# A GRU's input products: from seven products per four steps to 49 per eight

## The reference

```python
Xz, Xr, Xh = (x @ Wxg.T + bxg for g in "zrh")          # for all 512 steps
for t in range(512):
    Z = sigmoid(Xz[t] + H @ Whz.T + bhz)
    R = sigmoid(Xr[t] + H @ Whr.T + bhr)
    C = tanh(Xh[t] + (R * H) @ Whh.T + bhh)
    H = Z * H + (1 - Z) * C
    y[t] = H @ Whq.T + bhq
out = x + y
```

## Time and profile before

| | before |
|---|---|
| median of 3 runs, us | 2150.19 (2149.66 to 2152.09) |
| profiled execution: span, us | 2148.1 |
| PE busy | 2141.7 us, 100% |
| DVE busy | 1625.9 us, 76% |
| ACT busy | 914.6 us, 43% |
| POOL busy | 167.6 us, 8% |
| DMA | 62.20 MB, mean 29 GB/s |

### The profile page before, as it was taken

One profiled execution on the slowest core, in us unless ns is written; L12 is line 12 of the kernel. 1 busy time (PEld: TensorE's weight loads), 2 busy tenths in 40 slices (PEclk: granted clock), 3 DMA queues, 4 the chain that ended last, 5 costly groups with the idle time before them and its releaser, 6 DMA issues.

```text
span 2148.1 us, 179447 instructions
## 1 busy us (share of the span) xinstructions
PE 2141.7 (100%) x78028; PEld 2128.3 (99%) x78028; DVE 1625.9 (76%) x9472; ACT 914.6 (43%) x5118; POOL 167.6 (8%) x524
## 2 busy tenths in 40 slices
PE   9999999999999999999999999999999999999999
PEld 7999999999999999999999999999999999999998
DVE  5777777777777777777777777777777777777777
ACT  3444444444444444444444444444444444444443
POOL 1000000000000000000000000000000000000000
PEclk9999999999999999999999999999999999999999
DMA  4100010001000000000000100010001000010000
GB/s 155 29 24 24 26 29 24 24 24 31 24 24 24 29 26 24 24 26 29 24 24 26 29 24 24 25 30 24 24 24 30 25 24 24 26 29 24 24 26 27
DMA packets 111618, 62.20 MB, mean 29 GB/s; under 512 B 28786, under 2 KB 110834, under 8 KB 110834
## 3 DMA queue, kind: packets, MB, share of 16 engines
q1 hardware_dynamic: 111600, 61.98, 9.8%
q10 hardware_dynamic: 4, 0.02, 0.0%
HBM read 45.17 MB, written 16.78 MB: 29 GB/s over the span
## 4 chain that ended last, share of the span: by engine, by line
PE 99%; DMA 0%; DVE 0%; issue 0%; ACT 0%; POOL 0%; SPq 0%; DVEq 0%; POOLq 0%
PE gates L417 62%; PE p_bank L339 15%; PE gates L339 12%; PE y_bank L347 9%; PE p_bank L448 0%; PE gates L547 0%; DMA y_io<-in_x_res 0%; PE y_bank L540 0%; PE p_bank L540 0%; DMA out<-y_io 0%; DVE scanned L708 0%; DVE pre_t L644 0%; DVE wq_sums L698 0%; DVE y_io L648 0%; ACT scan_on L629 0%
## 5 line engine op out<-in xcount | busy, mean ns | idle before, releaser
L417 PE MATMUL gates<-wh,scanned 128*16 128x128 f32 x32768 | 1009.6, 273 | 1.5 <-DVE scanned L708 1.5
L417 PEld LDWEIGHTS gates<-wh,scanned 128*16 128x16 f32 x32768 | 933.4, 104 | 3.8 <-DVE scanned L708 1.3
L644 DVE STREAM_TRANSPOSE pre_t<-gates 128x32 f32<-128x32 f32 (+2 forms) x3584 | 617.1, 216 | 183.8 <-PE gates L417 139.3
L417 PE MATMUL gates<-wh,reset_state 128*16 128x128 f32 (+1 forms) x16384 | 562.0, 273 | 0.2 <-issue 0.2
L417 PEld LDWEIGHTS gates<-wh,reset_state 128*16 128x16 f32 (+1 forms) x16384 | 445.1, 103 | 0.5 <-issue 0.3
L614 ACT ACTIVATE r_gate<-pre_t 128x16 f32<-128x16 f32 (+1 forms) x1536 | 234.5, 215 | 408.4 <-DVE pre_t L644 408.4
L629 ACT ACTIVATE scan_on<-pre_t 128x16 f32<-128x16 f32 (+1 forms) x1536 | 236.4, 218 | 263.9 <-DVE pre_t L644 263.9
L339 PE MATMUL p_bank<-t,s 128*32 128x192 f32 x6096 | 333.9, 326 | 0.3 <-issue 0.3
L708 DVE TENSOR_TENSOR_SCAN scanned<-scan_by,scan_on 128x32 f32<-128x32 f32 x2048 | 299.3, 208 | 28.5
L617 ACT ACTIVATE scan_by<-pre_t 128x64 f32<-128x64 f32 x512 | 143.0, 279 | 263.9 <-DVE pre_t L644 263.9
L769 DVE TENSOR_TENSOR scan_on<-z_gate,scanned 128x64 f32<-128x64 f32 x512 | 120.8, 236 | 173.8 <-ACT z_gate L618 173.8
(11 more groups left out here) (77 smaller groups left out, 1538.5 us busy)
## 6 DMA issues: line engine op xcount, KB each, us to landing
y_io<-in_x_res SPq DMA_DIRECT2D x256, 64.0 KB, 1.9
out<-y_io SPq DMA_DIRECT2D x256, 64.0 KB, 1.6
xr<-in_x_t SPq DMA_DIRECT2D x127, 128.0 KB, 2.0
x_b<-in_x_t SPq DMA_DIRECT2D x127, 32.0 KB, 1.7
wx_v<-in_w_xv SPq DMA_DIRECT2D x1, 1536.0 KB, 6.5
wx_u<-in_w_xu SPq DMA_DIRECT2D x1, 1536.0 KB, 9.0
wh<-in_w_hr SPq DMA_DIRECT2D x1, 1024.0 KB, 10.7
wh<-in_w_hz SPq DMA_DIRECT2D x1, 1024.0 KB, 13.8
```

The costliest lines, as they stand in the source:

```text
L417: mm = nc.tensor.matmul(gate_rows(g, par, slice(Q * j, Q * j + rows)), of, w, start=False, stop=(m == G - 1), skip_group_check=True)
L644: nc.vector.transpose(flat(pre_t[g][:, a:b]), gate_part(g, par, a, b)).then_inc(done, 1)
```

## The change

A turn becomes eight steps (four pairs); 64 turns, of which two at the start and two at the end are unrolled on every engine, TensorE too, and 60 run in the loop. The x parts of a turn come from two levels of the scheme: seven products of blocks at the outer level, each again seven (49 block products, `x_products`), each over one m of 128 and 96 columns, four matmuls. The blocks 1, 2, 4 (`FIRST`) of the outer products are made in steps 4 to 7 of a turn, the others (`SECOND`) in steps 7 to 4 of the next; the results are used a turn later. The partial sums of the outer level pass through four banks by ACT copies (`start_a`, `a_to_b`, `d_to_b`, `d_to_c`, `z11_first` and so on; 14 per turn), DVE adds four (`z22_first`, `z12_first`, `z22_second`, `z12_second`, 288 or 384 columns). The inner level is put together on GpSimd from SBUF: 21 additions per turn (`combine_11`, `combine_21` of 96 elements, `combine_x2` of 192), next to four sums of x of 128 elements (`x_sum`) and four of 224 (`x_sub_sum`). ACT then copies the four pairs' parts to the gate banks (`put_u`, 256 columns, `put_v`, 128). Every GpSimd sum is issued behind a wait for a DVE event: the scans of a step (`after_state`), the state sums (`after_sums`), the third reset product (`after_reset`) or the kept product (`after_kept`). Gates lie in two banks for R and H (`u_bank`) and one for Z of both pairs (`v_bank`). The first eight pairs (16 steps) have plain products (`plain`), two gaps per pair. The 21 summed weight blocks of DVE (`sub_sum`) and 7 of GpSimd (`w_sub3`) are made during turns 0 and 1. The ten `keep_busy` matmuls between the first products are gone. SP loads 256 KB of x per turn of eight steps in one transfer.

```diff
-    W = P + P // 2
-    CW = G * W
...
+BLOCK = 96
+HALF = 2 * BLOCK
+COLS = 2 * HALF
...
-            turn(0, first=True, last=False)
-            with eng.Fori(1, turns - 1) as i:
-                turn(i, first=False, last=False)
-            turn(turns - 1, first=False, last=True)
+            turn(0)
+            turn(1)
+            with eng.Fori(2, turns - 2) as n:
+                turn(n)
+            turn(turns - 2, begins=False)
+            turn(turns - 1, ends=False, begins=False)
...
+            def x_sub_sum(n, k):
+                x = x_all[:, 0:7].rearrange("p s (i j q) -> p s i j q", i=2, j=2)
+                a0, a1, b0, b1 = (x[:, :, i, j, :] for i in range(2) for j in range(2))
+                s = {m: x_sub[:, m - 1] for m in range(1, 5)}
+                if n == 1:
+                    pool.wait_ge(s_ready[3], k + 1)
+                    pool.wait_ge(s_ready[4], k + 1)
+                    if not isinstance(k, int) or k > 0:
+                        pool.wait_ge(p4d_done, k)
+                    nc.gpsimd.tensor_tensor(s[1], b0, b1, ALU.add).then_inc(x_sub_made, 1)
...
+            def combine(op, made, z, x, k):
+                pool.wait_ge(made, 7 * k + op - 1) if op > 1 or not isinstance(k, int) or k > 0 else None
+                of = {1: (x(0, 0), z(1), z(2)), 2: (z(6), z(1), z(6)), 3: (z(3), z(5), z(3)),
+                      4: (x(0, 1), z(6), z(3)), 5: (z(7), z(6), z(7)), 6: (x(1, 0), z(7), z(4)),
+                      7: (x(1, 1), z(7), z(5))}[op]
+                nc.gpsimd.tensor_tensor(*of, ALU.add).then_inc(made, 1)
...
+                elif before:
+                    after_sums(2 * n)
+                    combine_x2(6, n - 2)
+                    combine_x2(7, n - 2)
+                    after_reset(t)
+                    combine_21(3, n - 2)
+                    after_kept(t)
+                    combine_21(4, n - 2)
+                    after_state(t + 1)
+                    combine_21(5, n - 2)
+                    combine_21(6, n - 2)
+                    after_reset(t + 1)
+                    combine_21(7, n - 2)
...
+                if begins:
+                    after_state(t + 5)
+                    x_sub_sum(1, n)
+                if ends:
+                    after_state(t + 5)
+                    combine_x2(1, n - 1)
+                    after_reset(t + 5)
+                    combine_x2(2, n - 1)
...
+            def x_products(to, a, blocks, only=None):
+                x, w = X_OF[a], W_OF[a]
+                x_raw = x_all[:, x].rearrange("p (i j q) -> p i j q", i=2, j=2)
+                for at, b in enumerate(blocks):
+                    if only is not None and at not in only:
+                        continue
+                    of = {1: x_raw[:, 0, 0], 2: x_raw[:, 0, 1], 4: x_raw[:, 1, 1], 3: x_sub[:, 3, x],
+                          5: x_sub[:, 0, x], 6: x_sub[:, 1, x], 7: x_sub[:, 2, x]}[b]
+                    by = {1: lambda: w_block(w, 0, 0), 2: lambda: w_block(w, 1, 0), 3: lambda: w_block(w, 1, 1),
+                          4: lambda: w_summed(4, w), 5: lambda: w_summed(1, w), 6: lambda: w_summed(2, w),
+                          7: lambda: w_summed(3, w)}[b]()
+                    for j in range(G):
+                        mm = nc.tensor.matmul(to[Q * j:Q * (j + 1), BLOCK * at:BLOCK * (at + 1)], of, by[:, j, :],
+                                              start=False, stop=True, skip_group_check=True)
...
+                    if s8 == 0 and ends:
+                        pe.wait_ge(z22a_out, n)
+                        x_products(a_bank, 4, FIRST).then_inc(p4a_done, 1)
+                        pe.wait_ge(b_put_d, n)
+                        if second:
+                            pe.wait_ge(w_sub3_made, 5)
+                        x_products(d_bank, 6, SECOND).then_inc(p6d_done, 1)
+                    elif s8 == 1 and ends:
+                        x_products(b_bank, 2, SECOND).then_inc(p2d_done, 1)
+                        pe.wait_ge(c_put_d, n)
+                        x_products(d_bank, 7, SECOND, (0,))
...
+                    elif s8 == 7 and begins:
+                        x_products(c_bank, 3, FIRST, (2,)).then_inc(p3a_done, 1)
+                        pe.wait_ge(b_started_a, n + 1)
+                        if first:
+                            pe.wait_ge(w_sub_made, 18)
+                        x_products(b_bank, 5, FIRST).then_inc(p5a_done, 1)
+                        pe.wait_ge(d_started, n + 1)
+                        pe.wait_ge(x_sub_made, 4 * n + 4)
+                        if first:
+                            pe.wait_ge(w_sub3_made, 1)
+                        x_products(d_bank, 1, SECOND).then_inc(p1d_done, 1)
...
+                    if s == 0 and (not static or n >= 2):
+                        put_v(par, x_part(p, n))
+                    if s == 0 and static and 1 <= 4 * n + p < 7:
+                        if 4 * n + p > 0:
+                            act.wait_ge(plain_done, 4 * n + p)
+                        put_u(1 - par, bias_rows)
+                        put_v(1 - par, bias_rows)
+                    if s8 == 0 and ends:
+                        p5_out_first(n - 1)
+                        d_to_b(n - 1)
+                    elif s8 == 1 and ends:
+                        d_to_c(n - 1)
...
+            def z22_first(k):
+                dve.wait_ge(p7a_done, k + 1)
+                dve.wait_ge(p5a_out, k + 1)
+                read_x2(k)
+                nc.vector.tensor_tensor(z_place(3, 0, 3), a_bank[:, 0:n_first], p5_first[:], ALU.add
+                                        ).then_inc(z22a_out, 1)
...
```

More of the change, by code:

```diff
@@ new lines, in keep_busy, with plain_in_gap @@
+                    nc.tensor.matmul(a_bank[Q * j:Q * (j + 1), :], zeros[:, 0:Q], zeros[:], start=True, stop=True)
+            def plain_in_gap(s8, t):
+                q = t // 2 + 1
+                if q >= 8:
+                    return
+                pe.wait_ge(z_turned, t + 1)
+                if q == 1 and t == 0:
+                    plain(1, 1, (0, 1))
+                    return
+                if q == 1:
+                    plain(1, 1, (2, 3)).then_inc(plain_done, 1)
+                    return
+                pe.wait_ge(u_put[q % 2], q // 2)
+                pe.wait_ge(v_put[q % 2], q // 2)
+                pe.wait_ge(x_rest_loaded, 16 if q < 4 else 32)
+                mm = plain(q, s8 % 2, range(G))
+                if s8 % 2 == 1:
+                    mm.then_inc(plain_done, 1)
@@ L537, in _ @@
             pe.wait_ge(zeros_ready, 1)
[L538 removed]
+            for to in (y_bank, c_bank, d_bank):
                 for j in range(G):
@@ L622, in turn @@
                         nc.scalar.copy(q16[:], y_bank[:, Q16_AT:Q16_AT + YW]).then_inc(q16_copied, 1)
-                    elif c == 1 and not last:
-                        if not first:
-                            act.wait_ge(ub_put, i)
-                        fill_p5()
                     for h, (a, b) in enumerate(PARTS):
@@ L712, in renew, with turn @@
                 mm.then_inc(state_ready[h], 1)
-            def turn(i, first, last):
-                for c in range(4):
-                    t = 4 * i + c
+            def turn(n, ends=True, begins=True):
+                static = isinstance(n, int)
+                first, second = static and n == 0, static and n == 1
+                last = not ends
+                ends = ends and not first
+                for s8 in range(8):
+                    odd, c = divmod(s8, 4)
+                    i, t = 2 * n + odd, 8 * n + s8
                     par, s = divmod(c, 2)
+                    end = last and odd == 1
+                    begin = first and odd == 0
                     old = state_before(c)
-                    if c == 0 and not first:
+                    if c == 0 and not begin:
                         state_sums(i)
-                    elif c == 1 and not first:
-                        put_ub(i)
-                    elif c == 2 and first:
+                    elif c == 2 and begin:
                         dve.wait_ge(q6_done, 1)
```

894 lines of the change are left out of this document (583 added, 311 removed).

## The result

The changed kernel takes **3002.73 us** (median, 3000.73 to 3004.05) against 2150.9 of the kernel before beside it: ratio **1.396 [1.394, 1.398]**, 852 us slower, where 405 slower was forecast. The profiled execution has a span of 2998.8 us at a mean granted clock of 0.932, where before had 1.00.

The account below looks back on a forecast made before the run. TensorE's records times columns bound the kernel, then its code loads. Span 2148.1 - 59 + 1 + 7 + 4 = 2101 with kept code, + 444 + 8 = 2553 with loads, plus 2.1 to the median: 2555 us, range 2102 to 2740.

Parts of the forecast that it names:

- The code: TensorE's loop body of 11 packets is loaded anew each pass: 7.4 us per body, +444 us over 60 bodies.
- Eleven need 36.3 us: TensorE's loop body: eleven code packets at 3.3 us each, where the body's work needs 32.2 us.
- another 3.3: TensorE's branch back aims at replaced code with nothing asked for ahead: one more load of 3.3 us per pass.
- Unrolled turns, +8: The four unrolled turns on TensorE load 42 packets of code: +8 us.
- +4: First sixteen steps: DVE's weight sums between its transposes delay H's transposes and others, +4 us (1 to 10).
- +7: Last eleven steps lose their products but must keep 1.05 us per gap: shortfalls sum to +7 us.
- Products, -59: TensorE's x products: 392 records of 96 columns replace 224 of 192 per eight steps, 583 to 524 us, -59.
- ScalarE hidden, transfers hidden: ScalarE's 22 copies per eight steps and SP's 256 KB x loads per body hide behind other work, costing nothing.
- GpSimd: Sums after the state sums (steps 0 and 4) delay DVE's reset products: 0.5 us per body, uncounted under code loads.
- A (2103): Whole kernel: code is kept and GpSimd's sums hold no one, 2103 us; chance 0.16.
- B (2134): Steps 0 and 4: code is kept, GpSimd's sums hold DVE's reset products, 31 us, giving 2134 us; chance 0.22.
- C (2277 to 2301): TensorE's loop: loads are just in time and only the branch back costs, 2277 to 2301 us; chance 0.12.

Follow-up runs that it names:

- loop of narrow records: No GRU computed: TensorE alone runs 16 passes of ten packets of 64-column matmuls on zeros; 175 packets in 619.3 us.
- loops of zeros: No GRU computed: TensorE alone runs loops of 16 passes of matmuls on zeros, varied in code size and columns; 3.54 us per packet with 64 columns.
- fitted half turn: Changed kernel, TensorE looping over four steps, branches picking x products, head at packet start, two y products left out: 2189.89 us, ratio 1.019.
- doubled loop: Kernel before with TensorE's loop written as two turns per pass, same instructions in the same order: 2575.91 us, ratio 1.198.
- small loop: No GRU computed: TensorE alone, 2.5 packets of code with a branch skipping 128 instructions every pass; 3 packets in 16 passes.

## Why the prediction was wrong, point by point

- **What bounds the kernel**: right; TensorE's records in order, then its code.
- **The code**: the mechanism was right, its size was the error. Forecast: 11 packets of 3.3 us and one blind load of 3.3 at the branch back, 39.6 us per pass. Measured: 13 packets, 46.9 us. The step that failed is "Eleven need 36.3 us", with the branch back's "another 3.3": these two terms are 439 of the 448 us that were missing. By the runs: the body's own 11 packets make 40.4 us (3.67 each), 4.1 more than forecast; the branch back without a named target adds a twelfth and 2.2 us, 1.1 less than forecast; the head's place near the end of a packet adds a thirteenth and 4.3 us, for which the sum had no term. (Taken in the other order the named target is worth 2.8 us and the head's place 3.8.) So the packet was sized 0.4 us low, 3.3 for 3.67 (3.54 in the loop of narrow records), the packets were not counted by where the body begins, and the branch was priced too high. The 7 packets that could be proved kept turned out to be all that is kept whole: 1,780 instructions stay, 1,816 don't. In the loops of zeros the loads are hidden, but for one wait of some 2.5 us per pass, where a packet of code is 5.2 us of work, and set the pace, 3.54 us each, where it is 1.8.
- **The granted clock**: put at nothing without a reason; the sum took waits as lost time only. Alone it costs at most 1.6 us behind 6.2 us of idle. In the changed kernel it is part of the 2.2 and 4.3 us; how much of them is not separated, since slower records also give the loads time to catch up.
- **Unrolled turns, +8, with +4 and +7 for start and tail**: measured on the fitted half turn, whose steady passes are even with before (33.21 against 33.18 us). Of the 38 us between the spans these make 2; 36 are left, where 19 were forecast. The seventeenth step starts at 114.39 us there and at 87.73 in the kernel before, 26.7 later; the loop's first passes, which have yet to load its seven packets, cost 6.6 more; the last two turns cost 3. An estimate from the records: some 9 of the 26.7 are block products that start early, and the tail should have given these back. The changed kernel waits 0.25 to 0.72 us for most packets of turns 0 and 1 (eight waits, 4.2 us, from 56 to 88 us); how the rest splits stays open.
- **Products, -59**: a record of 96 columns is right (20.7 ns forecast; 32 records of the changed kernel, first fence, in 0.66 us), the gain isn't. With kept code a pass takes 33.21 us, not 32.2. The chain of the fitted half turn shows why:

```profile
1540.63 0.66 PE b_bank L520 x32
```

```profile
1515.88 0.15 issue
1516.03 1.07 PE u_bank L614 x32
...
1522.21 1.08 PE u_bank L614 x32
...
1524.34 0.87 PE u_bank L614 x32
...
1532.26 0.33 issue
1532.59 1.07 PE u_bank L614 x32
```

The two branch backs wait 0.15 and 0.33 us, and by the chain the 32 records behind each take 1.07 us instead of 0.87: 0.88 us in all. With GpSimd's 0.18 that is about the 1.0. The H group at 1522.21, which has no y product in front of it, takes 1.08 us in the same way; four such groups per pass give back the 0.9 us of the four missing y products.

- **ScalarE hidden, transfers hidden**: right; in mid-run neither is named among TensorE's waits, with kept code either.
- **GpSimd**: a 192-element sum was estimated at 0.6 us and took 594 ns (below, from 1000 to 2500 us); 0.5 us per pass was taken, 0.28 and 0.18 measured. As forecast, no cost of it shows under the loads: the changed kernel's reset products last 178 and 193 ns (178 and 194 before) and end 2.1 us of TensorE's waits in all; no run took the sums out there. The reading of the earlier trace rows, that DVE's sum was held until GpSimd's ended, was too strong: held until 31.30 and then 0.38 us long it would have taken 0.62 us, and it took 0.52.

```profile
L314 POOL TENSOR_TENSOR x_parts<-z_of 128x192 f32<-128x192 f32 x130 | 77.2, 594 | 163.7 <-DVE h_sums L991 107.0 <-DVE reset_state L1124 54.1
```

- **Rivals**: A (2103) and B (2134) assumed kept code, which 10.9 packets exclude; and with kept code the half turn still has 2190, of which its second branch back per eight steps makes some 20 to 30. So a gain is not shown even then. C (2277 to 2301) missed the waits inside the body.
- **What would show it**: queue 8 at 700 packets, 822 came; idle 7 us per pass, 10 came, the longest at the loop's start, as forecast.

The sign was right, and for the reason given, which was no luck; it had a chance of 0.62. The range ended 263 us short: both its ends varied the time of a packet and neither the count of packets.

## What to carry to other kernels

Count the instructions of a loop body on its engine, control included, and compare with what the trace shows kept. On TensorE seven packets of 256 instructions stayed in these runs and eight didn't. The straight bodies of 9.6 and 10.9 packets lasted as long as the packets they drew, 3.5 to 3.7 us each, whatever the arithmetic saved. For short records a packet of code is less work (128 records of 20.7 ns are 2.6 us) than its own load, so unrolling twice as far can cost more than the products it saves. If a body must be over the limit, the head at the start of a packet and a named branch target gave back 386 us of the 852 here, but not the sign.

## What the runs showed of the hardware that I had not expected

- 7 packets kept, 8 reloaded whole (9 packets a pass): the step is sharp, 64 instructions were worth 970 us. A loop with branches only 24 instructions over it loaded 9 packets in every second pass.
- The branch back to code that is gone showed two waits in a row (3.34 and 2.71 us) as the loop stood, with ten records between them, and one (3.13) with its target at the start of a packet.
- The granted clock went to its lower level, 0.50, behind idles of 6.20 us (no code load) and of 2.70 us (the doubled loop), and stayed at 1.00 from 100 to 2500 us in the kernel whose waits at the head were 1.13 to 1.73 us there.
- A forward branch within kept code cost no load of its own: 3 packets came in the 16 passes of the small loop, and 9 from 1000 to 2000 us in the fitted half turn, which takes some 240 branches there. With eight of them per eight steps, for which up to 0.8 us had been estimated, the trace shows no wait but 0.15 and 0.33 us at the two branch backs, and 0.01 us in front of four H groups.
